# A causal attention and feed-forward layer on one core: the first stage regrouped by token chunks with its normalisation on GpSimd, and turned maxima and masks moved within the attention groups

## What is computed

```python
x  = hidden_states                       # 2048 tokens x 512, f32
xn = (x - mean) / sqrt(var + 1e-5)       # per token
q, k, v = split(xn @ w_qkv.T)            # 16 heads of 32
scores = where(causal, q @ k.T / sqrt(32), -max)
attn   = softmax(scores) @ v
ffn    = (gelu(xn @ Wg.T) * (xn @ Wu.T)) @ Wd.T   # 4096 wide; weights from 4-bit codes and scales
out    = x + attn @ w_o.T + ffn
```

## Time and profile before

| | us |
|---|---|
| median of three runs | 1986.68 |
| the profiled execution | 1986.45 |
| its span, first to last instruction | 1984.6 |
| TensorE busy | 1874.5 (94%) |
| VectorE, ScalarE, GpSimd busy | 1129.9, 698.7, 339.1 |
| first matmul of the projection | 53.84 |
| last matmul of the projection starts | 186.99 |
| first matmul of attention | 200.08 |
| output projection starts | 870.75 |

### The profile page before, as it was taken

How to read it: one execution, slowest core, us unless ns; L and a number is a source line. 1 busy time by engine, 2 the same in 40 slices (tenths; PEclk the granted TensorE clock), 3 DMA queues, 4 the chain that set the end, 5 groups by cost and what they waited for, 6 DMA issues and landing times.

```text
span 1984.6 us, 23894 instructions
## 1 busy us (share of the span) xinstructions
PE 1874.5 (94%) x8448; PEld 1328.4 (67%) x8448; DVE 1129.9 (57%) x1706; ACT 698.7 (35%) x1112; POOL 339.1 (17%) x339
## 2 busy tenths in 40 slices
PE   2997799999999999989999999999999999999997
PEld 2786454454444444435888888888888888888886
DVE  7220566555555565643865666566756676567643
ACT  3221245555555555521322332232322332223321
POOL 0001200111111101100222222222222222222221
PEclk9999699999999999999999999999999999999999
DMA  4663603134044140033101110111011100110002
GB/s 148 233 196 113 140 7 80 34 78 84 17 84 83 28 81 17 15 131 112 41 15 32 32 32 0 32 32 32 0 32 32 32 10 22 32 32 0 0 1 85
DMA packets 88857, 109.31 MB, mean 55 GB/s; under 512 B 44248, under 2 KB 60632, under 8 KB 85008
## 3 DMA queue, kind: packets, MB, share of 16 engines
q1 hardware_dynamic: 88784, 108.39, 20.2%
HBM read 75.09 MB, written 29.59 MB: 53 GB/s over the span
## 4 chain that ended last, share of the span: by engine, by line
PE 55%; DVE 0%; ACT 0%; POOLq 0%; issue 0%; POOL 0%
PE p_gate L50 6%; PE p_gate L48 6%; PE p_gate L49 6%; PE p_out L48 6%; PE p_out L50 6%; PE p_out L49 6%; PE p_up L50 6%; PE p_up L48 6%; PE p_up L49 6%; PE p_out L1101 1%; PE p_gate L1101 1%; PE p_up L1101 1%; DVE acc L1036 0%; POOLq L792 0%; DVE inter L1016 0%
## 5 line engine op out<-in xcount | busy, mean ns | idle before, releaser
L551 ACT ACTIVATE e_sb<-p_st 128x512 f32<-128x512 f32 (+3 forms) x640 | 297.3, 548 | 280.0 <-PE p_st L706 145.7
L604 DVE TENSOR_REDUCE max_part<-p_s 128x1 f32<-128x512 f32 x384 | 241.6, 683 | 108.7 <-PE p_s L680 108.4
L680 PE MATMUL p_s<-k_stack,q_stack 96*128 96x512 f32 (+3 forms) x640 | 232.9, 414 | 42.5 <-ACT q_stack L540 21.0
L727 PE MATMUL p_o<-e_sb,v_stack 128*33 128x512 f32 (+5 forms) x1280 | 251.0, 535 | 0.0
L706 PE MATMUL p_st<-q_stack,k_stack 128*128 128x512 f32 (+3 forms) x640 | 235.2, 406 | 6.7 <-ACT e_sb L551 4.9
L1016 DVE SCALAR_TENSOR_TENSOR inter<-inter,gate 128x1024 f32<-128x1024 f32 x64 | 78.4, 1225 | 255.2 <-ACT inter L932 254.6
L960 POOL TENSOR_SCALAR poly<-poly 128x1024 f32<-128x1024 f32 x64 | 71.2, 1113 | 875.8 <-ACT poly L927 875.8
L600 DVE CUSTOM_DVE_ANT_0 masked_scores<-p_s,score_mask 128x128 f32<-128x128 f32 (+3 forms) x256 | 119.6, 486 | 158.1 <-PE p_s L680 157.0
L48 PE MATMUL p_out<-i_hi,w_hi 128*128 128x512 f32 x512 | 200.0, 391 | 3.1 <-DVE acc L1036 3.1
L50 PE MATMUL p_out<-i_hi,w_lo 128*128 128x512 f32 x512 | 199.8, 390 | 0.0
L49 PE MATMUL p_out<-i_lo,w_hi 128*128 128x512 f32 x512 | 199.7, 390 | 0.0
(11 more groups left out here) (103 smaller groups left out, 2616.6 us busy)
## 6 DMA issues: line engine op xcount, KB each, us to landing
q_stack<-qk_scratch SPq DMA_DIRECT2D x48, 256.0 KB, 7.4
k_stack<-qk_scratch SPq DMA_DIRECT2D x48, 256.0 KB, 8.6
qk_scratch<-out_hi SPq DMA_DIRECT2D x32, 256.0 KB, 2.6
qk_scratch<-out_lo SPq DMA_DIRECT2D x32, 256.0 KB, 3.3
scales<-in_gate_up_s SPq DMA_DIRECT2D x128, 64.0 KB, 2.3
x_sb<-in_x SPq DMA_DIRECT2D x4, 1024.0 KB, 11.9
xn_lo_scratch<-xn_lo_made SPq DMA_DIRECT2D x1, 4096.0 KB, 13.3
v_scratch<-out_v SPq DMA_DIRECT2D x16, 256.0 KB, 2.0
```

The costliest lines, as they stand in the source:

```text
L551: nc.scalar.activation(e_sb[:, x % E_BUFS, :, 0:w], p_st[:, x % ST_BUFS, :, 0:w], ACT.Exp, scale=SCALE).then_inc(exp_done, 1)
L604: nc.vector.reduce_max(part, p_s[:, slot[n] % S_BUFS, 0:w], AX.X).then_inc(maxed, 1)
L680: nc.tensor.matmul(p_s[:, slot[n] % S_BUFS, 0:w], q_stack[p % PB][a][0:ROWS, i * P:(i + 1) * P], k_stack[p % PB][a][0:ROWS, b * W:b * W + ...
L727: last = nc.tensor.matmul(p_o[a * VW:a * VW + width, q0:], v_stack[p % PB][:, kt, a, 0:width], e_sb[:, x % E_BUFS, a if PH == 2 else 0, 0: ...
```

## The change

In the first stage, GpSimd normalises (L163 of the new file), SyncE loads in the order x0, w0, w1, x1, x2, x3, w2, and the projection goes chunk by chunk: TensorE starts on the eight q and k units of the first 512 tokens once these are turned. The next chunk's statistics stand behind the chunk's first unit, its 16 transposes behind the fifth (`TURN_BEHIND`). The 4 MB store stands behind the stores of q and k. In attention, the turned maxima stand behind the group's `scores_t` pieces and seven eighths of its units, ahead of the products, on TensorE, and behind all eight exponentials on ScalarE; the first pair has the lead of one group too. In diagonal groups two pieces are scored and then their two masks follow. The first group gets 20 units. `join_parts` follows its last unit instead of the group's end.

```diff
@@ norm_and_project, SyncE
-            for i in range(LOADS):
...
-            sp.wait_ge(xn_lo_made, TT)
-            sp.dma_start(xn_lo_scratch, xn_lo[:, :, :].bitcast(F32)).then_inc(xn_lo_stored, 16)
+            load_x(0)
+            load_w(0)
+            load_w(1)
+            for i in range(1, LOADS):
+                load_x(i)
+            load_w(2)
             for u in range(UNITS):
+                if u == UNITS_QK:
+                    sp.wait_ge(xn_lo_made, TT)
+                    sp.dma_start(xn_lo_scratch, xn_lo[:, :, :].bitcast(F32)).then_inc(xn_lo_stored, 16)
...
-                    ot, tc = divmod(u, TC)
+                    tc, ot = divmod(u, OT)
@@ GpSimd
+            for i in range(LOADS):
+                pool.wait_ge(rstd_made, i + 1)
+                for tt in range(i * PER, (i + 1) * PER):
+                    nc.gpsimd.tensor_scalar(x_sb[:, tt, :], x_sb[:, tt, :], mean_var[:, tt, 0:1],
+                                            rstd[:, tt:tt + 1], ALU.subtract, ALU.mult).then_inc(xn_made, 1)
@@ ScalarE; VectorE has norm, weights_lo and tokens_lo at the same places
+            root(0)
+            weights_hi(0)
+            tokens_hi(0)
+            weights_hi(1)
             for u in range(UNITS):
...
+                    if ot == NORM_BEHIND and tc + 1 < TC:
+                        root(tc + 1)
+                    if ot == TURN_BEHIND and tc + 1 < TC:
+                        tokens_hi(tc + 1)
+                    if u == V_WEIGHTS_BEHIND:
+                        weights_hi(2)
@@ TensorE
+            transposes(0)
             for u in range(UNITS):
-                if u % (KT * TC) == 0:
-                    pe.wait_ge(w_lo_made, u // (KT * TC) + 1)
+                tc, ot = divmod(u, OT)
+                if u < UNITS_QK and ot == 0:
+                    pe.wait_ge(xn_lo_made, (tc + 1) * PER)
+                if u in (0, KT):
+                    pe.wait_ge(w_lo_made, u // KT + 1)
...
+                if u < UNITS_QK and ot == TURN_BEHIND and tc + 1 < TC:
+                    transposes(tc + 1)
@@ attention
-    UNITS_FIRST = 12
+    UNITS_FIRST = (20, 12)
-    FIRST_LEAD = 0
...
-                TURNS[max(-1, -1 if p == 0 and r < 2 else wanted - (FIRST_LEAD if p == 0 else TURN_LEAD))].append((p, r, a))
+                TURNS[max(-1, -1 if p == 0 and r < 2 else wanted - TURN_LEAD)].append((p, r, a))
...
-        ring += TURNS[k] + units_of(k)
+        units = units_of(k)
+        ring += units[:7 * len(units) // 8] + TURNS[k] + units[7 * len(units) // 8:]
@@ ScalarE
-                for t in TURNS[k]:
-                    if t[0] == 0:
-                        max_row(*t)
                 for n in range(3):
                     exps(x + n)
-                for t in TURNS[k]:
-                    if t[0] > 0:
-                        max_row(*t)
                 copy_out_before(k)
                 for n in range(3, GS * PIECES):
                     exps(x + n)
+                for t in TURNS[k]:
+                    max_row(*t)
@@ TensorE
+            def mask_t(x):
+                if piece(x)[0] < NSTEP:
+                    nc.tensor.matmul(p_st[:, x % ST_BUFS, 0, 0:P], ident[:, :], mask_k[:, :], start=False,
+                                     stop=True).then_inc(st_ready, 1)
...
+                if DIAG[(GS * k + LEAD) % NS]:
+                    for n in (0, 2, 4, 6):
+                        scores_t(x + n)
+                        scores_t(x + n + 1)
+                        mask_t(x + n)
+                        mask_t(x + n + 1)
+                        for part in {0: (0, 1, 2), 2: (3,), 4: (4, 5), 6: (6,)}[n]:
+                            some_units(part, 8)
+                else:
...
                 for t in TURNS[k]:
                     turn_max(*t)
-                for n in range(3):
-                    scores_t(x + n)
...
                 for g in range(GS * k, GS * k + GS):
                     product_v(g)
                 some_units(7, 8)
```

More of the change, by code:

```diff
@@ L155, in root, with weights_hi, tokens_hi @@
                 nc.scalar.activation(std[:, cols], var_eps[:, cols], ACT.Sqrt).then_inc(std_made, 1)
[L157 to L164 removed]
+            def weights_hi(i):
+                act.wait_ge(w_loaded[i], 16)
+                nc.scalar.activation(w_hi[:, :, i * H:(i + 1) * H], w_sb[:, :, i * H:(i + 1) * H],
+                                     ACT.Copy).then_inc(w_hi_made, 1)
+            def tokens_hi(i):
                 for tt in range(i * PER, (i + 1) * PER):
@@ L222, in _, with transposes @@
                                         out_hi[:, u % SLOTS, :].bitcast(F32), ALU.subtract).then_inc(lo_made, 1)
+                tc, ot = divmod(u, OT)
+                if ot == NORM_BEHIND and tc + 1 < TC:
+                    norm(tc + 1)
+                if ot == TURN_BEHIND and tc + 1 < TC:
+                    tokens_lo(tc + 1)
+                if u == V_WEIGHTS_BEHIND:
+                    weights_lo(2)
         @block.tensor
         def _(pe):
-            pe.wait_ge(ident_made, 2)
-            for tt in range(TT):
-                pe.wait_ge(xn_made, tt + 1)
-                if tt >= 2:
-                    pe.wait_ge(xn_lo_made, tt - 1)
-                for kt in range(KT):
-                    par, half = divmod(kt, 2)
-                    first = 2 * P * half + par
-                    last = nc.tensor.transpose(pt[:, tt % 2, kt * P:(kt + 1) * P],
-                                               x_sb[:, tt, first:first + 2 * P - 1:2], ident[:, :])
-                last.then_inc(transposed, 1)
-            pe.wait_ge(xn_lo_made, TT)
-            for u in range(UNITS):
-                if u % (KT * TC) == 0:
-                    pe.wait_ge(w_lo_made, u // (KT * TC) + 1)
+            def transposes(i):
+                for tt in range(i * PER, (i + 1) * PER):
+                    pe.wait_ge(xn_made, tt + 1)
+                    if tt >= 2:
+                        pe.wait_ge(xn_lo_made, tt - 1)
+                    for kt in range(KT):
+                        par, half = divmod(kt, 2)
+                        first = 2 * P * half + par
+                        last = nc.tensor.transpose(pt[:, tt % 2, kt * P:(kt + 1) * P],
+                                                   x_sb[:, tt, first:first + 2 * P - 1:2], ident[:, :])
+                    last.then_inc(transposed, 1)
+            pe.wait_ge(ident_made, 2)
+            transposes(0)
+            for u in range(UNITS):
+                tc, ot = divmod(u, OT)
+                if u < UNITS_QK and ot == 0:
+                    pe.wait_ge(xn_lo_made, (tc + 1) * PER)
+                if u in (0, KT):
+                    pe.wait_ge(w_lo_made, u // KT + 1)
+                if u == UNITS_QK:
+                    pe.wait_ge(w_lo_made, 3)
                 if u >= SLOTS:
@@ L694, in scores_t @@
             def scores_t(x):
-                g, heads = piece(x)
+                g, (a,) = piece(x)
                 if g >= NSTEP:
@@ L701, in scores_t @@
                 if kt == 0:
-                    pe.wait_ge(max_rows, turn_index[p, qc, heads[-1]] + 1)
+                    pe.wait_ge(max_rows, turn_index[p, qc, a] + 1)
                 if x >= ST_BUFS:
                     pe.wait_ge(exp_done, x - ST_BUFS + 1)
-                for n, a in enumerate(heads):
-                    last = nc.tensor.matmul(p_st[:, x % ST_BUFS, n, 0:W - q0],
-                                            k_stack[p % PB][a][:, kt * P:(kt + 1) * P],
-                                            q_stack[p % PB][a][:, qc * W + q0:(qc + 1) * W], start=True,
-                                            stop=not DIAG[s])
-                if DIAG[s]:
-                    for n, a in enumerate(heads):
-                        last = nc.tensor.matmul(p_st[:, x % ST_BUFS, n, 0:P], ident[:, :], mask_k[:, :], start=False,
-                                                stop=True)
-                last.then_inc(st_ready, 1)
+                last = nc.tensor.matmul(p_st[:, x % ST_BUFS, 0, 0:W - q0], k_stack[p % PB][a][:, kt * P:(kt + 1) * P],
+                                        q_stack[p % PB][a][:, qc * W + q0:(qc + 1) * W], start=True,
+                                        stop=not DIAG[s])
+                if not DIAG[s]:
+                    last.then_inc(st_ready, 1)
+            def mask_t(x):
+                if piece(x)[0] < NSTEP:
+                    nc.tensor.matmul(p_st[:, x % ST_BUFS, 0, 0:P], ident[:, :], mask_k[:, :], start=False,
+                                     stop=True).then_inc(st_ready, 1)
             def product_v(g):
@@ L737, in _ @@
             pe.wait_ge(filled, NF)
-            for x in range(LEAD * PIECES):
+            for x in range(0, LEAD * PIECES, 2):
                 scores_t(x)
+                scores_t(x + 1)
+                mask_t(x)
+                mask_t(x + 1)
             pe.wait_ge(o_cleared, 1)
```

70 lines of the change are left out of this document (28 added, 42 removed).

## The result

The change makes the kernel faster: median 1940.2 us (1939.9 to 1941.45, four runs) against 1985.88 (1982.99 to 1987.85, four runs) of the kernel before on the same chip; ratio 0.9772, 95% interval 0.9761 to 0.9784. That is 45.7 us less where 57.4 were forecast.

| | before | after | change | forecast |
|---|---|---|---|---|
| first matmul of the projection | 53.84 | 22.73 | -31.1 | -34.8 |
| from there to the first of attention | 146.24 | 161.46 | +15.2 | +11.4 |
| attention, to the output projection | 670.66 | 641.24 | -29.4 | -33.8 |

The account below looks back on a forecast made before the run. TensorE was taken as the bound, except for its late start and stalls inside attention. From 1986.45 us, 23.4 less in the first stage and 33.8 in attention gave 1929.2, stated as 1929.0; own range 1921 to 1937, wider range 1919 to 1941.

Parts of the forecast that it names:

- rival 4: First stage: GpSimd too slow; at 2.8 us a tile TensorE waits before each of three chunks: 1950 us; chance 0.03.
- The start at 19.0: First stage: the first projection matmul starts at 19.0 us instead of 53.84, 34.8 earlier.
- I take 0.55, as the same operation: First stage: GpSimd normalises a tile of 512 columns in 0.55 us, priced from its other scalar operation; far end 1.2.
- The 0.55 that it adds for the exclusion: First stage: one tile's time added to the start because VectorE's weight split and GpSimd's normalisation exclude each other.
- Bursts of 3.7: Projection: three chunks' transposes each cost TensorE 3.7 us, between 3.3 and 4.1; 11.1 in all.
- rival 1: Projection: the clock falls at each chunk's transposes, each fall costing 1.7 to 3.4 us: 1934 to 1939; chance 0.17.
- v's stores at 0.3: Projection: the 4 MB store ahead of v's stores costs 0.3 us, at worst 1.5.
- Turned maxima, 0.95 a group: Attention: removing the stall behind the turned maxima gains 0.95 us in each of 28 groups, 26.7 in all.
- Rival 2: Attention: stalls only move, giving back half of the 26.7 us, 0.45 a group: 1942; chance 0.13.
- The first pair: Attention's beginning: two waits gain 3.4 and 2.9 us, regained clock 4.0; early turned pairs cost 1.2, changed unit counts 1.0.
- Grouped masks at 0: Attention's diagonal groups: scoring two pieces before their masks changes 0 us for 32 groups, between -0.3 and +0.3 each.
- Last pair: End of attention: grouped masks cost 1.0 us in the last pair's groups without units, where nothing fills the wait.

Follow-up runs that it names:

- experiment 7: The run e8: the changed kernel with GpSimd's normalisation written as multiply and add; 1931.47 us, ratio 0.9732.
- e8: Changed kernel, but GpSimd normalises by multiply and add, both by pointer, with a shift made by VectorE, instead of subtract and multiply; 1931.47 us, ratio 0.9732.
- e11: As e8, but attention's first group takes 16 units instead of 20; 1935.92 us, ratio 0.9751.
- e3: Changed kernel with each mask right behind its own piece again instead of grouped; 1939.76 us, ratio 0.9772.
- e9: As e8, but in diagonal groups only the first two masks stand behind both pieces, the others single, and the units are spread; 1923.4 us, ratio 0.9685.
- e6: Changed kernel with v's weights split behind the 22nd unit instead of the 18th, away from GpSimd's tiles; 1936.68 us, ratio 0.9754.
- e5: Changed kernel with all normalisation back on VectorE, behind each part's statistics, instead of on GpSimd; 1934.24 us, ratio 0.9734.
- e10: As e8, masks in twos, but in diagonal groups the units stand earlier among the pieces; 1927.5 us, ratio 0.9708.
- e12: As e9, with units at the same places, but every mask single, right behind its own piece; 1926.85 us, ratio 0.9708.

## Why the prediction was right, and where it was off

The call (faster) and the two mechanisms held: TensorE starts early because the projection goes by chunks, and the stalls behind the turned maxima are gone. The amount was 11 us off. It lies within the range of 1919 to 1941 by 0.8 us, outside the forecast's own 1921 to 1937, and that is in part luck: a GpSimd tile of 2.07 was beyond every bound of the forecast but rival 4's 2.8, which had a chance of 0.03. By its steps, from the spans and starts of the profiled executions:

- **The start at 19.0** came at 22.73. The step that failed is "I take 0.55, as the same operation" for a tile on GpSimd: it is 2.07 (experiment 7 shows that the operation pair, not the pointers or the stage, makes it so), outside even the far end of 1.2. With 0.77, or with VectorE doing it, the start is 18.5 to 18.6, so the rest of that sum was sound, and 0.5 too careful. The 0.55 that it adds for the exclusion was put on the wrong engine: VectorE's split kept its 2.29, and GpSimd's tile lost 1.6. (In the earlier trace rows VectorE's operation ends 1.08 behind GpSimd's, not 0.95.) Reading "the same operation" from a row that shows only its type was the mistake: the row is multiply and add with constants.
- **Bursts of 3.7** were 3.41, 3.42 and 5.83 (sum 12.7 against 11.1). Undisturbed they are 3.33, the lower bound. The third was rival 4's mechanism at a smaller price, and behind it rival 1's: at half clock a projection matmul takes 0.43 instead of 0.227, and ten of them stand between 95.32 and 99.5, 2.0 us.
- **v's stores at 0.3**: right. ScalarE's third copy of v waits for the stores, as foreseen, and TensorE then for that copy's slot; v's 192 matmuls take 43.6 us from first start to last in the change and 43.7 in e8, against 43.3 before.

```profile
143.14 1.21 ACT L207 ACTIVATE out_v<-pj 128x512 f32<-128x512 f32 x2 [9.59 <-DMA v_scratch<-out_v]
```

- Stage one in all: 23.4 less forecast, 15.9 measured (200.08 to 184.19), 25.2 in e8 (to 174.84).
- **Turned maxima, 0.95 a group.** Over the groups 10 to 69, of which 24 have turned maxima, the time fell from 469.7 to 449.4 us: 20.3, or 0.84 a group, where 22.8 was forecast. The stalls went as a whole; what the step left out is what is late in the new order (0.44 for the sixth piece in the timeline above), of which 0.11 a group is net. Rival 2 said that 0.45 would come back.
- **The first pair**: forecast 3.4 + 2.9 + 4.0 - 1.2 - 1.0 and two of the 0.95, 10.0 in all. Up to the first products it took 4.3 more (32.9 to 37.2, 20 units and half clock), over the groups 0 to 9 13.1 less (96.9 to 83.8): 8.8. The falls of the earlier trace rows are gone, and e11 shows that this hangs on the 20 units: with 16 the wait and the half clock are back. The 4.0 for the clock was itself misread: the earlier trace rows have TensorE busy for 5.66 and 3.50 us, half of which is 4.6.
- **Grouped masks at 0**: e3 bears out the number. But it is 0 only against this one alternative, and as a sum of 2.2 gained in the steady groups and 1.4 lost in the last pair. Both orders were poor, and e9's mixture is 8 us better; that the two waits could be had down together was not seen.
- **Last pair**: 0.9 less forecast (two stalls less 1.0), 0.4 measured (71.1 to 70.8 from group 70 to the output projection).

Attention in all: 8.8, 20.3 and 0.4, with the rounding 29.4, against 33.8. Of the 11.9 us by which the spans miss the sum, 7.5 lie in the first stage and 4.4 in attention. What e6, e5 and e8 give back in the first stage (3.9, 8.6 and 9.4 us) is what the GpSimd tile and its collision cost. By the spans they are 4.0, 6.4 and 11.5 ahead; the rest is where the clock falls and comes back: e5 loses 2.4 in attention, and e8 gains 1.3 there, as it has one fall near attention's end where the change has two. TensorE: Matmul & The Clock Gate of the Trainium skill, section "Part 4: PE-mode transpose", says that the full clock does not engage for transposes, and had made rival 1 the forecast; these runs do not bear it out as a rule for each burst: 3.33 to 3.5 us with 16 transposes left the clock at 1.00 in every kernel here, and only bursts lengthened to 5.6 and 5.8 us by waits were followed by 0.50.

Open: why one turn group in four (the one of 664.81 above, 8.52) gained nothing in e9, and why the clock comes back 2.5 us or more later in e5, e10 and e12 than in the other runs with 20 units. Also not shown is the cause of 2.07 against 0.77: the runs tell which pair of operations is slow, not why.

## What to carry to other kernels

Before work moves to another engine, price it from a row with the same operations, not only the same instruction type, and try the algebraic form that this engine does fast: here multiply and add in place of subtract and multiply, a factor of 2.7. Put a VectorE operation that reads two SBUF tensors where GpSimd has nothing urgent. When reordering removes a stall, read which engine is then late by tenths of a microsecond, and space the filler work between the pieces that wait for it; these small places were worth a quarter of the whole reordering of attention here (7.5 us against 29.4). And before a difference of 1 or 2 us is put down to an edit, look where the granted clock fell and rose in both traces.

## What was not expected of the hardware

- GpSimd's scalar operation on 128x512 f32 took 2.07 us with subtract and multiply by pointer, 1.92 with constants, 0.77 with multiply and add by pointer; the earlier trace rows have 1.05 for twice the columns, multiply and add with constants.
- A GpSimd tile that began beside VectorE's 2.29 us subtraction of two SBUF tensors took 3.68 and 4.2 us instead of 2.07, and 2.8 instead of 0.77. VectorE's, begun while a tile was running, took 2.29 (1.51 us behind the tile's start), 2.34 (0.56), 2.58 (0.33) and 2.62 (0.13).
- Attention's first 30 to 40 us were at half clock in all kernels; when the full clock came back differed by up to 10 us between them.
